# Graph attention and four row normalisations on one core: the scaling reads its factors from PSUM bank M1, and the first and the last steps are rearranged

## What is computed

```python
x = _layernorm(x + attention(x, adj))          # 4 heads of 16
x = _layernorm(x + _L1_gnn_ref(x, adj))        # (A + I) x / degree
x = _layernorm(x + _L2_gnn_ref(x, adj))        # A (x w) + bias
x = _layernorm(x + _L3_gnn_ref(x, adj))        # 1 where (A x) > 0.5, else 0

def _layernorm(x, axis=-1, eps=1e-05):
    m = jnp.mean(x, axis=axis, keepdims=True)
    v = jnp.var(x, axis=axis, keepdims=True)
    return (x - m) / jnp.sqrt(v + eps)

# attention; scores are f_self . f_other per head
masked = a_h * scores
masked = jnp.where(masked >= 0, masked, 0.2 * masked)
masked = masked / jnp.sqrt(jnp.float32(ATT))
masked = masked + jnp.where(a_h == 0, jnp.float32(-1000000000.0), jnp.float32(0.0))
attn = jax.nn.softmax(masked, axis=-1)
```

## Time and profile before

| | |
|---|---|
| median of 3 runs | 1761.11 us (1760.62 to 1762.89) |
| profiled execution | 1762.62 us, its span 1760.8 us |
| PE, DVE, ACT, POOL busy | 1454.2, 1384.5, 1241.6, 1089.5 us (83, 79, 71, 62% of the span) |
| mean granted TensorE clock | 0.912 |
| L922, the scaling | 28 instructions, 72.4 us |
| L837, VectorE's subtractions | 192 instructions, 283.2 us, mean 1475 ns |
| L403, GpSimd's subtractions | 384 instructions, 894.7 us, mean 2346 ns |

### The profile page before, as it was taken

The page is one execution under the profiler, slowest core; times in us unless marked ns, Lnnn a source line. Parts: engine busy times, 40 slices in busy tenths (PEclk is TensorE's granted clock), DMA queues, the critical chain, the costliest instruction groups (busy, mean ns, idle before and its releaser), DMA issues.

```text
span 1760.8 us, 22052 instructions
## 1 busy us (share of the span) xinstructions
PE 1454.2 (83%) x7728; PEld 718.8 (41%) x7728; DVE 1384.5 (79%) x1623; ACT 1241.6 (71%) x1475; POOL 1089.5 (62%) x581
## 2 busy tenths in 40 slices
PE   4487889898889889888889888988899987888745
PEld 3233334444444444444444443444444443344313
DVE  3567788878898778888888778987888788888654
ACT  2377878777687777777787777777687777777521
POOL 1056676676676666676576667776666766766642
PEclk9788989999899999999999999999999999999767
DMA  5413142122413133221522234130432214000000
GB/s 77 61 32 48 31 66 40 46 30 39 70 31 46 26 52 51 52 36 26 68 40 43 25 55 58 39 44 17 63 46 52 30 37 55 21 12 24 15 6 9
DMA packets 55067, 71.42 MB, mean 41 GB/s; under 512 B 21814, under 2 KB 42814, under 8 KB 54958
## 3 DMA queue, kind: packets, MB, share of 16 engines
q0 software_dynamic: 13824, 18.01, 13.7%
q1 hardware_dynamic: 41134, 52.01, 11.4%
HBM read 102.29 MB, written 3.26 MB: 60 GB/s over the span
## 4 chain that ended last, share of the span: by engine, by line
PE 45%; DVE 24%; issue 12%; ACT 11%; SPq 3%; POOL 3%; DMA 2%; ACTq 0%; POOLq 0%; DVEq 0%
PE M L586 11%; DVE RUN L823 9%; PE M L535 9%; PE Z L496 8%; PE Z L498 7%; ACT LS L677 6%; PE Z L509 4%; DVE LS L837 4%; ACT LS L685 3%; SPq L286 2%; DVE X L922 2%; POOL LS L403 2%; PE Z L596 2%; DVE RUN L820 2%; PE Z L657 2%
## 5 line engine op out<-in xcount | busy, mean ns | idle before, releaser
L403 POOL TENSOR_TENSOR LS<-LS,MB 125x1000 f32<-125x1000 f32 x384 | 894.7, 2346 | 489.4 <-DVE LS L837 334.8
L823 DVE TENSOR_TENSOR RUN<-Z,RUN 125x1000 f32<-125x1000 f32 x528 | 631.0, 1195 | 208.7 <-ACT LS L677 203.4
L677 ACT ACTIVATE LS<-Z 125x1000 f32<-125x1000 f32 x576 | 574.5, 998 | 262.0 <-PE Z L498 261.4
L685 ACT ACTIVATE LS<-LS 125x1000 f32<-125x1000 f32 x576 | 594.5, 1033 | 71.3 <-POOL LS L403 56.2
L496 PE MATMUL Z<-AT,BI 126*125 126x500 fp8e4 x1152 | 386.0, 418 | 140.1 <-DVE RUN L823 107.0
L535 PE MATMUL M<-LS,V 125*18 125x500 f32 x2304 | 326.7, 642 | 57.8 <-ACT LS L685 57.0
L498 PE MATMUL Z<-FS,FO 96*125 96x500 bf16 x1152 | 360.1, 395 | 0.0
L837 DVE TENSOR_TENSOR LS<-LS,MB 125x1000 f32<-125x1000 f32 x192 | 283.2, 1475 | 4.9 <-DMA MB<-row_maxima 2.8
L496 PEld LDWEIGHTS Z<-AT,BI 126*125 126x125 bf16 x1152 | 140.7, 146 | 282.9 <-DVE RUN L823 164.5
L498 PEld LDWEIGHTS Z<-FS,FO 96*125 96x125 bf16 x1152 | 165.5, 144 | 111.4 <-issue 21.3
L586 PE MATMUL M<-AT,XP 125*128 125x500 fp8e4 x756 | 206.8, 396 | 0.7 <-ACTq L735 0.7
(11 more groups left out here) (118 smaller groups left out, 1039.6 us busy)
## 6 DMA issues: line engine op xcount, KB each, us to landing
MB<-row_maxima SPq DMA_DIRECT2D x48, 488.3 KB
A<-in_adj_dram POOLq DMA_DIRECT2D x96, 183.1 KB, 4.8
FO<-PARTS SPq DMA_DIRECT2D x192, 46.9 KB, 2.1
FS<-PARTS SPq DMA_DIRECT2D x192, 46.9 KB, 2.1
XP<-in_x_dram SPq DMA_DIRECT2D x8, 375.0 KB
XA<-in_x_dram SPq DMA_DIRECT2D x8, 375.0 KB
out_dram<-X SPq DMA_DIRECT2D x7, 375.0 KB
row_maxima<-LMAX SPq DMA_DIRECT2D x48, 3.9 KB
```

The costliest lines, as they stand in the source:

```text
L403: nc.gpsimd.tensor_tensor(rows, rows, MB[:, u % 2, :, :], ALU.subtract).then_inc(sub_pool, 1)
L677: nc.scalar.activation(LS[:P, q % RL, :, :], banks("Z", q)[:P], ACT.Prelu, alpha=0.2).then_inc(bent, 1)
L685: nc.scalar.activation(rows, rows, ACT.Exp, scale=0.25).then_inc(exps, 1)
L823: nc.vector.tensor_tensor(run, z, run, ALU.max).then_inc(maxed, 1)
```

## The change

Middle: `scale` first copies the 12 factors of each partition from RSTD to M1[:, 0:12], waits for its own copy, and reads the factors from there; then it waits for its own end and releases the bank. The copy is a new user "S" of M1 in the list that sets TensorE's waits; `counted` numbers the users without it, for ScalarE's waits.

Start: the small weights, biases and XA are issued ahead of the features; WA and WV are issued by ScalarE; FS of heads 0 and 1 is issued by ScalarE beside SP's FO; each load of rows (XF and XA, in every graph) is split into 112 and 13 partitions; six of the seven memsets of AT go to GpSimd, with the loads of A8 between them behind all other constants; FE is made between the transpositions; the wait for the biases moves to the first `keep`.

End: the last unit's RUN is turned at step QN instead of QN + 1; the last 18 subtractions (e from DRAIN = 558 on) are all VectorE's; slices 0 and 1 of the last graph's first normalisation run at steps 594 and 596 within the loop; in the layers after it each slice's low part comes one slice earlier.

```diff
+DRAIN = QN - LAG
...
-CONSTS = 16
+CONSTS = 16 + RS - 1
...
+LAST_ROWS = QN + 18
...
+        def turned_at(q):
+            return NU - 1 if q == QN else unit_at(q, RT_AT) if q < QN else None
...
+            if layer_at(q, SCALE):
+                m1.append(("S", *layer_at(q, SCALE)))
...
+        def by_vector(e):
+            return e % TURN == TURN - 1 or e >= DRAIN
+        def by_dve(e):
+            return min(e, DRAIN) // TURN + max(e - DRAIN, 0)
         def by_pool(e):
-            return e // TURN * (TURN - 1) + min(e % TURN, TURN - 1)
+            return e - by_dve(e)
...
             def load_rows(b, dst, sem_):
-                sp.dma_start(dst.rearrange("p (s k) f -> p s k f", k=ST), x_v[b]).then_inc(sem_, 16)
+                for rows in (slice(0, 112), slice(112, P)):
+                    sp.dma_start(dst[rows].rearrange("p (s k) f -> p s k f", k=ST), x_v[b][rows]).then_inc(sem_, 16)
...
             load_rows(0, XF, xf_in)
-            sp.dma_start(WA[:, 0, :, :], wself.rearrange("h f o -> f h o")).then_inc(early_in, 16)
-            sp.dma_start(WA[:, 1, :, :], wother.rearrange("h f o -> f h o")).then_inc(early_in, 16)
-            sp.dma_start(WV[:, :, :], wv.rearrange("h f o -> f h o")).then_inc(early_in, 16)
-            load_features(0, 0)
-            load_features(0, 1)
             sp.dma_start(WW[0:F, 1, :], w2).then_inc(weights_in, 16)
             sp.dma_start(WW[F:2 * F, 1, :], w2).then_inc(weights_in, 16)
             sp.dma_start(B0[:, :, :].rearrange("p h o -> p (h o)"),
                          bias0.rearrange("a b h o -> (a b h o)").partition_broadcast(P)).then_inc(weights_in, 16)
             sp.dma_start(B2[:, :], bias2.partition_broadcast(P)).then_inc(weights_in, 16)
             load_rows(0, XA[:, :, :], xa_in)
+            sp.wait_ge(lo_ready, NS)
+            for h in range(2):
+                load_parts(FO[:, h, :], fo_in[0], 1, h)
+            load_features(0, 1)
             for q in range(END):
                 b, r = graph_at(q)
-                if unit_at(q, MAX_AT) is not None:
-                    spread_maxima(unit_at(q, MAX_AT))
+                if turned_at(q - 1) is not None:
+                    spread_maxima(turned_at(q - 1))
...
-            load(RA)
...
-            for t in range(RA + 1, RA + ST):
-                load(t)
...
+            for n in range(1, RS):
+                const(nc.gpsimd.memset(AT[96:P + 1, n, :, :, :].rearrange("p q n k -> p (q n k)").bitcast(f32), ONES8))
+                if n <= ST:
+                    load(RA + n - 1)
...
-            for c in range(NS):
-                features("FE", c, Z[:, c, 0], pre_xts[c]).then_inc(pre_fe, 1)
             for k in range(ST):
                 if k:
                     pe.wait_ge(at_ready, k)
                 turn_adj(k, M1)
+                if k < NS:
+                    features("FE", k, Z[:, k, 0], pre_xts[k]).then_inc(pre_fe, 1)
...
+            act.dma_start(WA[:, 0, :, :], wself.rearrange("h f o -> f h o")).then_inc(early_in, 16)
+            act.dma_start(WA[:, 1, :, :], wother.rearrange("h f o -> f h o")).then_inc(early_in, 16)
+            act.dma_start(WV[:, :, :], wv.rearrange("h f o -> f h o")).then_inc(early_in, 16)
...
+            act.wait_ge(lo_ready, NS)
+            for h in range(2):
+                for n, pair in enumerate(TERMS):
+                    act.dma_start(FS[n * D:(n + 1) * D, h, :], PARTS[h * D:(h + 1) * D, pair[0], :]).then_inc(fs_in[0], 16)
...
-            for n in range(RS):
+            for n in range(1):
...
+                if u == 0:
+                    dve.wait_ge(weights_in, 4 * 16)
...
             def scale(b, l):
+                dve.wait_ge(m1_read, order["S", b, l])
                 dve.wait_ge(rstd_ok, 4 * b + l + 1)
+                nc.vector.tensor_copy(M1[:P, 0:NT], RSTD[:, :]).then_inc(factors_in, 1)
+                dve.wait_ge(factors_in, 4 * b + l + 1)
                 if l == 0 and b:
                     dve.wait_ge(stored, 16 * b)
                 nc.vector.scalar_tensor_tensor(out=X[:, :, :], in0=Y[:, :, :], scalar=F ** 0.5,
-                                               in1=RSTD[:, :].unsqueeze(2).to_broadcast(bc3),
+                                               in1=M1[:P, 0:NT].unsqueeze(2).to_broadcast(bc3),
                                                op0=ALU.mult, op1=ALU.mult).then_inc(x_ready, 1)
+                dve.wait_ge(x_ready, 4 * b + l + 1)
+                dve.sem_inc(m1_read, 1)
...
-            dve.wait_ge(weights_in, 4 * 16)
+            dve.wait_ge(const_ok, CONSTS)
...
-            for l in range(4):
-                for c in range(NS):
-                    if l:
-                        add(l - 1, c)
-                    normalise(l, c)
-                    if c:
-                        scaled(l, c - 1)
-                    if c > 1 and l < 3:
...
+                if q == LAST_ROWS:
+                    for n in range(3):
+                        neighbours(B - 1, n)
+                    for c in range(NS - 1):
+                        normalise(0, c)
+                if q == LAST_ROWS + 2:
+                    for c in range(NS - 1):
+                        scaled(0, c)
+            normalise(0, NS - 1)
+            low_part(0, 0)
+            low_part(0, 1)
+            scaled(0, NS - 1)
+            low_part(0, NS - 1)
+            for l in range(1, 4):
+                add(l - 1, 0)
+                normalise(l, 0)
+                for c in range(1, NS):
+                    add(l - 1, c)
+                    centred(l, c)
+                    scaled(l, c - 1)
+                    summed(l, c)
+                    if l < 3:
+                        low_part(l, c - 1)
                 scaled(l, NS - 1)
                 if l < 3:
+                    low_part(l, NS - 1)
```

More of the change, by code:

```diff
@@ L172, in adj_resnorm @@
         rstd_ok = sem("rstd_ok")
+        factors_in = sem("factors_in")
         y_ready = sem("y_ready")
@@ L1024, in normalise, with summed @@
                 follow(c)
+            def summed(l, c):
+                rows = slice(ST * c, ST * (c + 1))
+                y, squares = Y[:, rows, :], SQ[:, rows, :]
                 step(c, nc.vector.tensor_tensor(squares, y, y, ALU.mult))
@@ L1044, in low_part @@
                                         ALU.subtract).then_inc(end_low, 1)
[L1046 to L1054 removed]
+            for c in range(NS):
+                rest(0, c, Z[:, c, 1], SPARE[:, c % 2, :])
+                low(0, c, SPARE[:, c % 2, :])
```

128 lines of the change are left out of this document (61 added, 67 removed).

## The result

| | before | after |
|---|---|---|
| median of 4 runs, us | 1760.86 (1760.32 to 1762.89) | 1689.47 (1682.54 to 1694.07) |
| profiled execution, us | 1762.62 | 1687.15 |
| its span, us | 1760.8 | 1685.3 |
| granted TensorE clock, whole span | 0.912 | 0.944 |
| start: to VectorE's first maximum, us | 60.6 | 37.7 |

The ratio is 0.9589, 95% interval [0.9553, 0.9626]: 4.1% faster. The forecast was 1678 us, range 1638 to 1722. The three stages gave 22.9, 34.4 and 18.2 us where 25, 39 and 19 were forecast. The stages and the last row of the table are those of one profiled execution each; the last row is added up from the clock records between the first and the last maximum. A second profile of the changed kernel (it stands among the experiments) has a middle of 1546.7 us, 154 us of it at the lower clock, so the middle is known to some 5 us only and its gain is 29 to 34 us.

A forecast was written before the change was run, and what follows sets the result against it. TensorE limits most of a graph, VectorE the four layer normalisations, with stalls at both ends. 1762.6 less 39 (middle), 25 (start), 19 (end) and 1.5 (profiled run to median) gives 1678 us, range 1638 to 1722.

The forecast's parts named there:

- The scaling: Middle, VectorE's scaling: 0.95 us plus a copy of 0.17, with waits 1.4 us instead of 2.6.
- Rival (a): Middle: the port wait moves into the copy, so the middle gains nothing and pays 11 us; 1728 us, chance 0.15.
- Direct gain: Middle: 22 us saved on VectorE's queue over 28 scalings, less 3 us for layer 0's bank, 19 us.
- clock 20: Middle: smaller TensorE gaps let its clock fall less often; 20 us, about a fifth of 95, bounds 0 and 95.
- Rival (b): Middle: the clock stays up nearly everywhere, 79 us saved there; 1638 us, chance 0.14.
- The inherited wait: Middle: VectorE's next subtraction waits for the same GpSimd instruction, so 0.74 us is saved at the traced place, not 1.2.
- M1 at layer 0: Middle: the feature matmul FE waits 1.1 us longer for the bank, mostly absorbed; 0.4 x 7 = 3 us charged.
- Rival (d): Middle: TensorE stands behind the scaling's hold of bank M1 at all 28 scalings, 85 us lost; 1802 us, chance 0.03.
- The start: Start: constants become what is late, at 32.4 us; first maximum at 35.5, 25 us saved, bounds 18 and 28.
- Rival (c): Start: the two DMA queues don't issue in parallel, 18.7 us saved instead of 25; 1684 us, chance 0.18.
- The end: End: earlier broadcast, VectorE's last subtractions, earlier normalisation and earlier low parts save 19 us, bounds 10 and 25.
- The surcharge for PSUM: Middle: the skill's extra fixed cost for reading PSUM, 28 x 62 cycles or 1.8 us, was left out of the sum.

The follow-up runs named there:

- the filling: Small matmuls of zeros in TensorE's gap after each scaling: 40 in the changed kernel with the old scaling, 0.9681; 32 in the changed kernel itself, 0.9595.
- the mean from PSUM: Changed kernel with the sums of layers 1 to 3 reduced into bank M1 and read there by the centring: 1686.54 us, 0.9569.

## Why the prediction was right, and where it was off

**The scaling: right, in mechanism and size.** 0.95 us, copy 0.17, no spread: as forecast from L909's minimum and L823's steadiness. Rival (a), the wait moving into the copy, falls with the copy's 163 to 175 ns in all 28 places. Reading the same factors from SBUF brings the wait back (0.9785), and with that any explanation by the new order falls.

**Direct gain 19 us, clock 20: the sum a little too high, the split not shown.** The middle gave 34.4 us instead of 39, and 29 by the second profile of the changed kernel. In the profiles the gains at the four scaling steps of a graph add up to 3.1 us (0.6, 0.9, 0.8, 0.9), or 22 us for seven graphs, which is the 22 of the sum; that leaves 7 to 12 us for the clock and everything else. A whole graph (mean of the third to the seventh) went from 203.3 to 197.9 us.

The weakest number of the prediction was the "about a fifth" for the clock: it meant 40 us less at the lower level, each worth half. Both factors were off, in opposite directions, and that the term came out near is luck. The time at the lower level fell by 77 us (217 to 140; 63 by the second profile), and behind the scalings by 91 (121 to 30): at three of the four places the low stretch is gone nearly everywhere, and it is left at step 65, where the gap stayed over 2 us. And each such microsecond is worth less than half: where the filling took 120 us away (222 to 102) the middle became 23.6 us shorter in the profiles and the median 16.5, that is 0.20 or 0.14 for each; between the kernels with the mean from PSUM, without and with the filling, it is 15.5 us for 71 (1545.5 to 1530.0; 160 to 89), 0.22. By these prices the clock is worth 11 to 17 us here, an estimate, since the filling costs something itself.

The medians can't split the gain either. The filled gap brings 16.5 us with the old scaling (0.9775 to 0.9681), and the new scaling with the gap filled brings 15 more (0.9681 to 0.9595); but in the other order the new scaling brings 33 (0.9775 to 0.9589) and the filling nothing. The intervals leave 6 to 8 us either way on each part, and the late scores of the filled kernels are in them.

Rival (b), the clock up nearly everywhere, asked for a middle 79 us shorter and a clock of 0.97. The two windows show 0.96 and 0.97, above the forecast's 0.94 to 0.95, and the whole middle 0.955; the time shows that the last 140 us at the lower level weren't taken away, and that those that were brought less than (b) counted.

**The inherited wait: right, and there is more of it.** L867's mean went up from 1.475 to 1.605 us. At the place of the earlier trace rows, copy and scaling take 1.16 us instead of 3.07, 0.15 go to the wait for the scaling's end, the subtraction takes 1.95 instead of 1.18, and the gap shrinks by 0.85; the prediction had 0.74 there. But the subtractions right behind the 27 scalings of the middle grew by 0.34 us on average (1.19 to 1.53), 9 us in all, while all 185 of the middle grew by 0.20 (1.45 to 1.64), 36 us in all. The rest is waiting at other places, which the sum didn't have. VectorE's busy time fell by 3.3 us only (1384.5 to 1381.2), for a time 71 us shorter. Nor did the prediction see that this subtraction is urgent: putting it off cost some 42 us.

**M1 at layer 0: 3 us charged, nothing visible.** FE waited 0.91 us for the scaling's release, as expected, and the fill behind it then waited only 0.31 us for VectorE:

```profile
880.74 1.08 PE L586 MATMUL M<-WV,YT 64*125 64x64 f32 x8 [0.91 <-DVEq L962]
...
883.14 0.66 PE L520 MATMUL Z<-AT,BI 126*125 126x500 fp8e4 x2 [0.31 <-DVE RUN L853]
```

The hold stands in place of a wait for VectorE. Rival (d) falls with it.

**The start: 22.9 instead of 25, by one mis-sized term.** The constants ended at 32.47 (forecast 32.4), but "this is what is late next" was wrong: the features were. Their 12 issues took 7.9 us (forecast 7.5), and from the last issue's end to the fill it took 5.1 us (4.7 to 6.2 in the eleven profiles with two queues) instead of the 2.4. (The 35.6 of one of them, the kernel with the mean from PSUM, isn't the forecast come true: its features were issued 1.8 us sooner.) Those 2.4 were read at the end of the old batch, where GpSimd's loads of A8 had nearly all landed; earlier in the same batch, with one queue but beside these loads, landing took up to 5.7 us (the FS issued at 28.20 landed at 33.91). With two queues the last features are issued in the middle of the loads of A8. From 21 to 35 us in the changed kernel (queue, packets and MB, share of the DMA engines' time; then size and median from issue to landing):

```profile
q0 software_dynamic: 563, 0.74, 64.3%
q1 hardware_dynamic: 555, 0.85, 19.7%
q10 hardware_dynamic: 384, 0.58, 14.9%
...
FO<-PARTS SPq DMA_DIRECT2D x18, 46.9 KB, 4.9
FS<-PARTS ACTq DMA_DIRECT2D x12, 46.9 KB, 5.0
```

q0 is GpSimd's queue, on which nothing but the loads of A8 runs here: they take 64% of the engines' time, and all the features together 35%. The loads of rows and weights that were moved ahead are over by then: between 14 and 19 us no DMA packet moves. With one queue (window 21 to 37) the medians are 3.4 us for FO and 2.8 for FS. The share of busy time of the DMA engines was 0.94 and 1.06 (the last three columns are clock, share and GB/s):

```profile
21.00:29.00 8.00, 6.57 (x25) 5.62 (x25) 2.44 (x5) 0.00 (x0) 4.35 (x5) 1.00 0.94 133
29.00:35.00 6.00, 0.36 (x1) 0.29 (x2) 0.22 (x1) 0.94 (x3) 3.23 (x3) 1.00 1.06 184
```

Full engines fit the longer landing; no run changed the loads of A8 alone, so this cause is argued and not shown. GpSimd's memset took 1.34 to 1.38 us where 1.8 was estimated, but the loads of A8 between them set the pace, so the sum stood.

Rival (c) falls as it was priced: two queues issued side by side at 0.63 and 0.66 us, where a single queue takes 3.75 / 6 = 0.63, and the 24 DMAs were issued in 7.9 us and not in 15. The total wouldn't have shown it, for 1689 us lies nearer to (c)'s 1684 than to 1678. The Trainium skill, "Perfetto Trace Analysis", section on HWDGE instructions, has the generator shared and locked while it is used. A lock held for the whole of an issue isn't what this trace shows: if issuing takes turns at all, it costs ScalarE's queue 0.03 us an issue. Whether something behind the issue is shared for a shorter time, no run here shows.

**The end: 18.2 instead of 19.** To the first L681 14.0 us were saved, where 1.7 + 7.3 + 5.1 = 14.1 were forecast; behind it 4.2 instead of 5.

**The surcharge for PSUM.** The Trainium skill, "VectorE: DVE Perf Modes", section on the TRN2 errata, has 120 cycles of fixed cost from PSUM and 58 from SBUF; that is, by an estimate from these two figures, 62 cycles more for each scaling. 953 ns from PSUM and SBUF against 957 at the least from two SBUF inputs, same line and shape: none is to be seen in the durations, and leaving it out was right. This pair is the better ground for it; L940 and L1020, which the prediction compared, are different operations.

## What to carry to other kernels

Where one line's durations spread while another of the same shape doesn't, look at which operands lie in SBUF and what GpSimd does at that moment: a VectorE operation with two SBUF inputs stood still for GpSimd's, and moving the small one of its two inputs to PSUM, for 0.17 us, freed it completely. A simple test is the time from the end of the GpSimd instruction to the end of VectorE's: where it is the same in all places, VectorE waited. Count as gain only what isn't inherited by the next two-input operation, and don't reorder that one without asking who reads its result. Price the clock apart from the work: filling TensorE's gap with matmuls of zeros gives a lower bound of what the clock is worth in a kernel, and may itself be a version to keep. Make the filling shorter than each gap that it stands in, or it holds up the work behind it. Read the landing time of a DMA in a stretch with the same transfers beside it as it will have after the change.

## What the runs showed of the hardware that was not expected

- TensorE, given 2.38 us of zeros to multiply in a gap of 3.5 us, kept its clock up behind it, and a kernel with nothing else changed ran 16.5 us (0.94%) faster.
- At steps 29 TensorE's gap went from 2.2 to 0.9 us or less, and the time at 1.2 GHz within 25 us behind the scalings there from 34 us to 0.6; at steps 65 it went from 3.5 to 2.7, and the time from 41 us to 24.
- A VectorE instruction with two SBUF inputs that met a running GpSimd instruction ended a fixed time after it: the scaling 0.81 to 0.83 us, in 28 of 28 places.
- A second DMA queue at the start moved the end of issuing by 7.3 us but the landing by only 3.9.
- The waits for GpSimd are not local: the put-off subtraction took 2.36 us behind a different GpSimd instruction, and putting it off behind each scaling cost more than the edit's whole gain in the middle.
- In its first four runs the changed kernel spread over 0.7% (1682.5 to 1694.1), and in four more over 0.1% (1689.7 to 1691.65); before spread over 0.15% in its first four, and over 0.5 and 0.6% in the runs beside the experiments (1759.1 to 1767.9, 1757.9 to 1768.2). What sets this was not looked into.
